# Row gathers by indirect DMA for experts 1 to 7, slot lists one expert ahead, and a reordered feed-forward and second norm

## The reference

```python
gate = fp4_linear(x, w_gate); y = fp4_linear(x, w_up)          # layer 0, feed-forward
h = silu(gate) * y
return fp4_linear(h, w_down)
...
h_t = dA_t * h + dBu_t; y = einsum('bdn,bn->bd', h, C_t)       # layer 1, scan over tokens
...
scores = softmax(einsum('bsd,ed->bse', x, router_w))           # layer 1, experts
gate_vals, sel_idx = top_k(swapaxes(scores, 1, 2), 129)
tokens = x[b_idx, sel_idx]
h = gelu(einsum('becd,edh->bech', tokens, w1) + b1)
y = einsum('bech,ehd->becd', h, w2) + b2
out = zeros_like(x).at[b_idx, sel_idx].add(y * gate_vals[..., None])
```

## Time and profile before

| | |
|---|---|
| median of 3 runs | 802.26 us (802.05 to 807.47) |
| the profiled execution | 803.25 us, its span in the trace 801.5 us |
| PE busy | 659.5 us, 82% of the span |
| DVE busy | 586.7 us, 73% |
| ACT busy | 499.6 us, 62% |
| POOL busy | 440.0 us, 55% |
| mean granted TensorE clock | 0.878 of full speed |

### The profile page before, as it was taken

How to read it: one execution, slowest core, us unless ns; L and a number is a source line. 1 busy time by engine, 2 the same in 40 slices (tenths; PEclk the granted TensorE clock), 3 DMA queues, 4 the chain that set the end, 5 groups by cost and what they waited for, 6 DMA issues and landing times. The chain is left out here.

```text
span 801.5 us, 9146 instructions
## 1 busy us (share of the span) xinstructions
PE 659.5 (82%) x3075; PEld 406.0 (51%) x3075; DVE 586.7 (73%) x794; ACT 499.6 (62%) x936; POOL 440.0 (55%) x246
## 2 busy tenths in 40 slices
PE   4847666598699999999987799999999960699993
PEld 2343444432455555655522445555555550688883
DVE  6794775464599999999754599999999859544331
ACT  3552332277789988889558799888988451222321
POOL 1236553100288988879600388989878524054636
PEclk9975788597599999999997599999999955799997
DMA  5000000000123332322100223222223251022313
GB/s 187 0 3 1 0 1 0 1 2 5 65 79 101 89 100 79 106 92 92 40 2 12 73 82 103 92 92 90 96 90 103 91 215 52 2 19 23 28 14 28
DMA packets 30334, 47.17 MB, mean 59 GB/s; under 512 B 3512, under 2 KB 12104, under 8 KB 29776
## 3 DMA queue, kind: packets, MB, share of 16 engines
q1 hardware_dynamic: 25600, 44.45, 17.0%
q0 software_dynamic: 4688, 2.13, 3.0%
HBM read 42.07 MB, written 4.49 MB: 58 GB/s over the span
## 5 line engine op out<-in xcount | busy, mean ns | idle before, releaser
L465 POOL TENSOR_TENSOR hc_all<-hs_all,c_row 128x1024 f32<-128x1024 f32 x88 | 207.3, 2367 | 141.8 <-DVE hs_all L1580 138.6
L1102 PE MATMUL ps<-hc_all,ident 128*128 128x512 f32 x512 | 240.0, 600 | 3.8 <-POOL hc_all L465 2.7
L1580 DVE TENSOR_TENSOR_SCAN hs_all<-da,ps 128x1024 f32<-128x1024 f32 x88 | 198.2, 2271 | 24.0 <-ACT da L763 15.7
L763 ACT ACTIVATE da<-big,a_neg 128x511 f32<-128x511 f32 x256 | 169.3, 709 | 32.0 <-DVE w_ffn L1580 28.9
L1102 PEld LDWEIGHTS ps<-hc_all,ident 128*128 128x128 f32 x512 | 90.3, 192 | 87.6 <-issue 74.2
L465 POOL TENSOR_TENSOR hc_all<-w_ffn,c_row 128x1024 f32<-128x1024 f32 x40 | 94.6, 2364 | 31.9 <-DVE w_ffn L1580 31.8
L1580 DVE TENSOR_TENSOR_SCAN w_ffn<-da,ps 128x1024 f32<-128x1024 f32 x40 | 91.4, 2285 | 4.2 <-ACT da L763 0.9
L519 POOL DMA_INDIRECT out<-hc_all,hs_all x32 | 49.4, 1544 | 51.8 <-issue 31.9
L1125 PE MATMUL ps<-ident,dbu 128*128 128x128 f32 x472 | 65.3, 284 | 8.8 <-ACT dbu L737 4.1
L1125 PEld LDWEIGHTS ps<-ident,dbu 128*128 128x128 f32 x472 | 56.1, 146 | 26.1 <-issue 15.9
L846 ACT ACTIVATE big<-ps,b 128x516 f32<-128x516 f32 x32 | 22.1, 691 | 52.0 <-PE ps L1275 52.0
(11 more groups left out here) (279 smaller groups left out, 1055.9 us busy)
## 6 DMA issues: line engine op xcount, KB each, us to landing
c_row<-c_rows SPq DMA_DIRECT2D x128, 256.0 KB, 3.1
tmpA<-w_in SPq DMA_DIRECT2D x2, 1024.0 KB, 7.0
tmpB<-w_in SPq DMA_DIRECT2D x2, 1024.0 KB, 9.8
x_tok<-x_in SPq DMA_DIRECT2D x2, 512.0 KB, 5.7
out<-x_tok SPq DMA_DIRECT2D x1, 1024.0 KB, 11.5
xm_rows<-xn SPq DMA_DIRECT2D x1, 1024.0 KB, 5.0
w_mod<-w_mod_in SPq DMA_DIRECT2D x2, 384.0 KB, 6.5
w_ffn<-w_ffn_in SPq DMA_DIRECT2D x1, 560.0 KB, 7.7
```

The lines of the kernel that those rows point to most:

```text
L465: nc.gpsimd.tensor_tensor(hc[:, n % 4, :, :], hs3[HS_BUF[n]].rearrange("p (i s) -> p i s", i=IC), c_row[:, n % 4, :].unsqueeze(1).to_broad ...
L763: ins = nc.scalar.activation(da[:, n % 2, i, 1:S], dtT[:, b, i, 1:S], ACT.Exp, scale=a_neg[:, l, i, n:n + 1])
L1102: mm = nc.tensor.matmul(ps[:, YS + i, :], ident[:], hc[:, n % 4, i, :], start=(n == 0), stop=(n == NS - 1))
L1580: v.tensor_tensor_scan(hs3[HS_BUF[n]], decay, pair.rearrange("p i s -> p (i s)"), 0.0, ALU.mult, ALU.add).then_inc(c_scan, 1)
```

## The change

1. For experts 1 to 7 the tokens of batches 2 and 3 (`BY_DMA`) come from `xm_rows` by two indirect DMAs on POOL, each of 128 rows of 512 bytes, into `x_rows_dma`, and PE transposes them, two float32 transposes in place of 24 bfloat16 matmuls. Batches 0 and 1, and all of expert 0, are gathered as before. POOL issues the two DMAs of expert e+2 ahead of the four scatters of expert e, and those of expert 1 and 2 ahead of expert 0's. `x_rows_dma` has two halves.
2. `slot_lists` is a function of its own. The list of expert 0 now stands ahead of gather(0), that of expert 1 ahead of hidden(0), and that of expert e+2 ahead of outputs(e); last_outputs(e) of experts 0 to 5 stands behind outputs(e).
3. Feed-forward: `hid` has three parts; `hidden_magnitudes(p-1)` stands behind the SiLU of pair p; `normalise_x(b+2)` moves to the even pair, `modulate_x` and `scales_x` to the start of a pair's turn; `add_down(p-3)` stands behind the multiply of pair p (before: `add_down(p-2)` behind `round_hidden(p-1)`).
4. Second norm: statistics, square root, reciprocal, normalisation and transposes go batch by batch, and batches 0 to 2 are placed among the last pairs of the feed-forward; batch 3's transposes stand behind the first half of the first Mamba projection, and its modulated copy behind the copies of that half.
5. Scan: state 1 of batch 0 is made by row in both Mamba layers; `turn(0, 1)` waits until `turn(0, 0)` was copied out of the one bank `OUT`, and `magnitude(3)` stands between the two copies.

```diff
-        hid = tmpB[:, 0:4 * FF].rearrange("p (h t f) -> p h t f", h=2, t=2)
+        hid = tmpB[:, 0:6 * FF].rearrange("p (h t f) -> p h t f", h=3, t=2)
...
-        BY_ROW = [0, 5, 8, 11, 14]
+        BY_ROW = [[0, 1, 5, 8, 11, 14] if g % B == 0 else [0, 5, 8, 11, 14] for g in range(L * B)]
...
+            def gather_rows(e):
+                pool.wait_ge(e_list, e + 1)
+                after(pool, e_gather, e - 1)
+                for j, b in enumerate(BY_DMA):
+                    nc.gpsimd.indirect_dma_start(x_rows_dma[:, e % 2, j, :], None, xm_rows,
+                                                 bass.IndirectOffsetOnAxis(slot_row[:, e, b:b + 1], 0)).then_inc(ld_rows[e % 2], 16)
+
             pool.wait_ge(stored, 48)
+            gather_rows(1)
             for e in range(E):
+                if e + 2 < E:
+                    gather_rows(e + 2)
...
                 nc.scalar.activation(silu_g[:, pair % 2, :, :], ps[:, GATE:GATE + 2, 0:FF], ACT.Silu).then_inc(f_silu, 1)
+                if pair:
+                    hidden_magnitudes(pair - 1)
...
+            down(2 * B - 2)
+            transpose_hidden(2 * B - 1)
+            transposed_second(0)
+            down(2 * B - 1)
+            transposed_second(1)
+            transposed_second(2)
...
                 if l == 0:
                     project_in(0, 0, 0)
+                    transposed_second(B - 1)
...
+                if e:
+                    pe.wait_ge(ld_rows[e % 2], 32 * ((e + 1) // 2 if e % 2 else e // 2))
+                    for j, b in enumerate(BY_DMA):
+                        mm = nc.tensor.transpose(ps[:, XG, b * P:(b + 1) * P], x_rows_dma[:, e % 2, j, :], ident[:])
...
-                if e < E - 1:
-                    pe.wait_ge(e_list, e + 2)
-                    last_outputs(e)
+                if e < E - 2:
+                    pe.wait_ge(e_list, e + 3)
+                    last_outputs(e)
...
                 dve.wait_ge(f_silu, pair + 1)
-                after(dve, f_htr, pair - 1)
+                after(dve, f_htr, pair - 2)
...
+                if pair >= 3:
+                    add_down(pair - 3)
                 dve.wait_ge(f_hid, pair + 1)
                 after(dve, q_h["q_done"], pair - 1)
                 scales(q_h, hid_flat(pair), 1 + pair % 2)
...
             for pair in range(2 * B):
...
+            add_down(2 * B - 3)
+            second_stats(0)
             round_hidden(2 * B - 1)
+            second_stats(1)
             add_down(2 * B - 2)
+            inverse(4, 0)
+            dve.wait_ge(mod_done, 3)
+            normalise_batch(0)
+            second_stats(2)
+            inverse(4, 1)
+            normalise_batch(1)
             add_down(2 * B - 1)
```

More of the change, by code:

```diff
@@ L205, in upto @@
         def upto(of, b, n):
-            return len(of) * b + sum(m <= n for m in of)
+            return sum(map(len, of[:b])) + sum(m <= n for m in of[b])
         def since(buf, n):
@@ L435, in _ @@
                     divide(q_x, b + 2, x_flat(b + 1), 0)
+                if pair % 2 and b + 2 < B:
+                    modulate_x(b + 2)
                 if pair < 2 * B:
@@ L611, in evacuate_x, with hidden_magnitudes @@
                 nc.scalar.copy(xqT[:, b % 2, :], ps[:, GATE, :]).then_inc(f_xqT, 1)
+            def hidden_magnitudes(pair):
+                after(act, q_h["q_rounded"], pair)
+                magnitudes(q_h, pair, hid[:, pair % 3, :, :], ps[:, MAG:MAG + 2, 0:FF])
             def evacuate_hidden(pair):
@@ L643, in _, with deviation, modulated_second @@
                     magnitudes(q_x, b + 2, x_flat(b + 1), mag_x)
[L644 to L646 removed]
+                if pair % 2 == 0 and b + 2 < B:
                     normalise_x(b + 2)
[L648 to L655 removed]
+                if pair >= 2:
+                    evacuate_hidden(pair - 2)
+            hidden_magnitudes(2 * B - 1)
+            def deviation(norm, b):
+                ts = slice(b * TB, (b + 1) * TB)
+                act.wait_ge(stat_ready, norm * NT + (b + 1) * TB)
+                nc.scalar.activation(std[:, ts], mv[:, ts, 1], ACT.Sqrt, bias=eps[:, 0:1]).then_inc(std_ready, 1)
+            def modulated_second(b):
                 act.wait_ge(norm_tr, B + b + 1)
@@ L1008, in _, with transposed_second @@
                     transpose_hidden(pair - 1)
-            down(2 * B - 2)
-            transpose_hidden(2 * B - 1)
-            down(2 * B - 1)
-            for b in range(B):
+            def transposed_second(b):
                 pe.wait_ge(xn_ready, NT + TB * (b + 1))
-                pe.wait_ge(f_x, 2 * B)
+                pe.wait_ge(f_hid, 2 * B)
                 for j in range(TB):
@@ L1150, in _ @@
                             row(b + 1, 0)
-                        if n in BY_TOKEN:
+                        if b == 0 and n == 0:
+                            turn(0, 1)
+                        if n in BY_TOKEN[l * B + b]:
                             increment(b, n)
```

183 lines of the change are left out of this document (91 added, 92 removed).

## The result

| | before | changed |
|---|---|---|
| median of the timed runs | 804.44 us (802.05 to 807.47) | 775.33 us (772.02 to 778.2) |
| the profiled execution | 803.25 us, span 801.5 | 776.74 us, span 774.8 |
| PE busy | 659.5 us | 642.5 us |
| DVE busy | 586.7 us | 589.9 us |
| ACT busy | 499.6 us | 496.1 us |

The changed kernel takes 0.9635 of the time before, 95% interval 0.9575 to 0.9694. It is faster by about 29 us in the medians; between the two profiled executions the span shrinks by 26.7, where 22 was forecast. The kernel before took 803.0 to 807.1 us on the chips of the experiments, so kernels from different experiments are compared here by their ratio to it on the same chip, given behind each time.

A forecast was written before the change was run, and what follows sets the result against it. PE bounds the experts, a ring of waits the feed-forward. Gains of 10 (experts), 9 (feed-forward and norm) and 3 (scan) make 22 off 803.25, 781.2; the median, 1.0 lower, gives 780.3 us, range 773 to 791.

The forecast's parts named there:

- Experts, PE's side: Experts: fewer gather matmuls and a closed hole shorten each turn by 1.73 us; after late starts, 10.0 us gained.
- Experts, POOL's side: Experts: six issues of 1.85 us take 11.1 per expert, yet POOL finishes at 769.2, before PE's 770.2; gain stays 10.0.
- 0.05 more: Experts: the 32-row gather beside picks took 1.59 us against 1.54 for a scatter alone, taken as the picks' cost.
- The rule that was set aside: Experts: the skill's statement that two-input VectorE and SBUF-reading GpSimd instructions exclude each other; the sum counted nothing for it.
- fourth rival: Experts: DVE's picks stop POOL 2.5 us every turn; experts lose 4 instead of gaining 10, 794 us; chance 0.07.
- the full rule: Experts: exclusion for whole instructions, POOL stopped for all four picks; six turns lose 15 us, less 1.0 of room.
- POOL as the bound: Experts: if 128-row gathers cost more to issue, 0.5 us extra each costs 5 us, 785; chance 0.12.
- The other rivals: Feed-forward gives nothing (790.5, chance 0.12); its clock stays up (774, 0.06); experts' rows land too late (803 or more, 0.05).
- Feed-forward: Feed-forward: removed waits shorten pairs 4 to 7 by 3.7 us and the batch ahead by 2.6; 6.5 taken.
- Second norm: Second norm: only batch 3 and part of 2 remain after feed-forward, 4.7 us less; 2.4 given back, net 2.3.
- Feed-forward and norm 9: Feed-forward and second norm together: 8.8 us reckoned, 9 taken as the gain.
- Scan: Scan starts: state 1 by row takes 1.70 us off ACT while DVE waits; 1.5 per layer, 3 in all.

The follow-up runs named there:

- picks_psum: Changed kernel with the picks of experts 2 to 7 reading slot numbers from PSUM, behind hidden's first matmuls: 777.29 us, 0.9644 of before.
- rows_three_best: Changed kernel with PSUM picks for experts 2 to 7, batch 3 ahead of the first projection, and three batches' rows by DMA: 777.6 us, 0.9697 of before.
- ff_mag_late: Changed kernel with the magnitudes of each pair back in that pair's own turn, three parts of hid kept: 776.49 us, 0.9674 of before.
- norm_b3_first: Changed kernel with batch 3's transposes ahead of the first projection and its modulated copy ahead of the projection's copies: 776.36 us, 0.9614 of before.
- after_again: The changed kernel itself, unaltered, in six timed runs and a second profile: 776.21 us, 0.9664 of before.
- rows_one: Changed kernel with only batch 3's rows fetched by DMA: 776.21 us, 0.9638 of before.
- rows_none: Changed kernel with no batch's rows fetched by DMA, slot lists still one expert ahead: 781.6 us, 0.968 of before.

## Why the prediction was right, and where it was not

The median of 775.33 lies in the range (773 to 791) and 5 us below the 780.3; the direction was right, and so was the mechanism of each part. One term was put at nothing and was not nothing: what DVE's picks cost POOL's issues. By the steps:

- **Experts, PE's side (forecast 10.0).** The turn shrank by 1.88 (12.06 to 10.18) where 1.73 was reckoned, in six turns 11.3. Expert 1's turn is 0.92 longer than the rest, with 0.71 of wait for its rows, against 0.5. hidden(0) starts 2.26 later behind the picks' start (9.08 instead of 6.82), against 1.65. The term that was missing is the seventh turn, 12.36 instead of 16.19: it saves 3.8 us and not 1.7, of which 0.4 are row and gate matmuls that no longer stand there and a part the clock: PE was granted 0.89 in that turn before and 1.00 in the changed kernel (windows, columns as in the earlier trace rows). The six turns' 11.3 less 0.9 for expert 1, less 2.3 for hidden(0), plus 3.8 make 11.9 in the first profile. In the second the same kernel gains 6.8; the forecast of 10.0 lies between the two.

```profile
765.22:781.41 16.19, 15.56 (x142) 13.72 (x140) 3.48 (x13) 4.14 (x10) 7.43 (x5) 0.89 0.18 17
```

```profile
741.28:753.64 12.36, 12.36 (x104) 10.92 (x103) 2.50 (x9) 4.14 (x10) 8.20 (x6) 1.00 0.29 33
```

- **Experts, POOL's side.** "An issue takes 1.54" was too much for a gather: 0.94 to 1.03. From the list of expert 2 to the last scatter of expert 5 the queue took 61.1 us (686.78 to 747.92) where 64.8 was reckoned. The price was that of a scatter, and the 32-row gather's 1.59 seemed to bear it out. That row was misread: in picks_psum, where DVE's picks begin 0.13 after it and not 0.07 ahead of it, the same gather takes 1.10 (timeline of POOL):

```profile
669.65 1.10 POOL L505 DMA_INDIRECT w_attn<-xm_rows,last_row  x1 [14.06 <-DVE last_row L1696]
```

So 0.5 of the 1.59 were already a wait for the picks: the first boundary between two of them comes 0.55 after the issue. "0.05 more" compared a gather that had waited with a free scatter.

- **The rule that was set aside** (fourth rival, 0.07). This is the step that failed: "By the trace the sum stays as it is". The runs show the rival's mechanism: a held issue lasts beyond the end of the picks, 1.6 to 2.4 us longer than a free one. It is not in every turn: an issue that gets in between two picks loses 0.1 to 0.2 us. So it costs 5 us in some executions and little in others, not the 14 of the full rule. That it did not cost more is in part luck: the 12 gathers were each about 0.5 cheaper than reckoned, and this room of some 6 us (an estimate) takes up most of the holds. The Trainium skill, "SBUF — State Buffer", section "Who interferes with whom", names the condition: two SBUF inputs on VectorE against a GpSimd operation that reads SBUF. The runs agree, 3.54 us beside such picks and 1.58 beside those with one input in PSUM. The same section also tells of a probe in which `tensor_tensor` did not stall a DMA; the picks are that operation, and here the issues beside them were held.
- **POOL as the bound** (0.12). Not in the changed kernel's first profile, by 2.94 us of idle ahead of L524; in the second it is, by the held issues and not by the gather's price, and in rows_three_best fully.
- **The other rivals.** The feed-forward gave more than its sum, and its clock did not stay up (mean 0.75 of full speed, 0.76 before). Apart from expert 1's 0.7 us, PE waited for rows only behind held issues, 1.5 us at each of two experts in the second profile.
- **Feed-forward (6.5).** Measured 7.9. The legs were 6.96, 9.72 and 5.41 against 7.45, 9.9 and 5.8; the batch ahead gave 3.0 (forecast 2.6), the first pairs 0.3. The sum was right and a little small. Of the reasons given, the SiLU behind the magnitudes was no limit in the first leg (ff_mag_late).
- **Second norm (4.7, then 2.4 given back).** Measured 5.3. In the changed kernel 5.7 were given back; 3.5 of them are the clock. The order of batch 3 cost 3.4 us net in norm_b3_first (the copy comes 0.7 later, the stretch behind it is 4.1 shorter), against the 2.4, with a part that can be the clock. "Feed-forward and norm 9" came out as 7.6.
- **Scan (3).** 7.04 us from the first scan's end to the second step against 7.3, and 4.3 in all, 4.1 alone.
- **What no step had:** 3.1 us in projections 1, from the clock; 0.8 ahead of the feed-forward, less than kernels with the same instructions differ by there (1.5); 1.0 lost at the end, which was not followed up.

Of the 4.7 us between the forecast span gain of 22 and the 26.7, then, 1.9 are the experts (in the lucky one of two executions), 1.3 the scans, 3.1 the clock of projections 1 and 0.8 the start, less 1.4 in feed-forward and norm and 1.0 at the end.

## What to carry to other kernels

Before an indirect DMA goes into a queue that is nearly full, look at what DVE does at the moment of its issue: an operation with two SBUF inputs can hold it to its end, and a queue without room hands that on to everyone who waits for it. One meeting in a trace does not price such a hold; compare an instruction with its own kind, free and beside the other engine. Where one execution gains more than the sum says, profile the same kernel twice, and compare the granted clock of the stretch, before a part is credited with it.

## What the runs showed of the hardware

- In the changed kernel the free issue of an indirect gather of 128 rows takes 0.94 to 1.03 us and that of a scatter with addition about 1.55 (up to 1.63); both with 0.30 before it. The number of rows matters little: 32 rows took 1.10 (gather, picks_psum) and 1.35 (scatter).
- Beside four picks of 0.62 us with two SBUF inputs, an issue took up to 3.54 (scatter) or 3.42 (gather) in after_again and ended 1.48 or 0.89 after the picks. DVE is not slowed: 2.49 in either case. With one input in PSUM (picks_psum): 1.58, picks 2.48.
- The same instructions ran in 41.9 or 38.4 us (projections 0, changed kernel and rows_one, granted clock 0.86 and 0.93) and in 42.9 or 39.9 (projections 1, rows_none and changed kernel, 0.91 and 0.98).
